# Cross attention: the attention result is split into two f16 parts by rows and transposed by the DMA crossbar, not by TensorE

## The reference, cut to what matters

```
q = x_norm @ wq.T ; k_new = x_norm @ wk.T ; v_new = x_norm @ wv.T
k = concat([ctx, k_new]) ; v = concat([ctx, v_new])
attn = softmax(q @ k.T * 512 ** -0.5)
out = attn @ v                    # (queries, 512)
x = x + out @ wo.T
```

## Time and profile before

| | |
|---|---|
| median of 3 runs | 1349.93 us (1348.22 to 1350.03) |
| the profiled execution | span 1349.0 us from first to last instruction |
| PE / DVE / ACT / POOL busy | 1327.4 / 1019.0 / 514.4 / 384.2 us |
| PE share of the span | 98% |
| mean DMA rate over the span | 90 GB/s |

### The profile page before, as it was taken

One profiled execution on the slowest core, in us unless ns is written; L12 is line 12 of the kernel. 1 busy time (PEld: TensorE's weight loads), 2 busy tenths in 40 slices (PEclk: granted clock), 3 DMA queues, 4 the chain that ended last, 5 costly groups with the idle time before them and its releaser, 6 DMA issues. The chain is left out here.

```text
span 1349.0 us, 23490 instructions
## 1 busy us (share of the span) xinstructions
PE 1327.4 (98%) x9232; PEld 773.9 (57%) x9232; DVE 1019.0 (76%) x2336; ACT 514.4 (38%) x1268; POOL 384.2 (28%) x304
## 2 busy tenths in 40 slices
PE   8999999999999999999999999999999999999998
PEld 6666666646666666666666666654444434444443
DVE  7444444269988888887888878858999798689594
ACT  4333333253333334343343334320001476666661
POOL 0000000012333222332223322313043296757571
PEclk9999999999999999999999999999999999999999
DMA  9555544541100220012210124155661000000002
GB/s 344 211 207 204 203 188 188 219 179 48 33 21 28 64 64 32 17 32 63 64 32 17 32 64 156 38 140 170 147 234 63 1 1 1 1 0 7 26 1 94
DMA packets 41766, 122.57 MB, mean 91 GB/s; under 512 B 4280, under 2 KB 6968, under 8 KB 34232
## 3 DMA queue, kind: packets, MB, share of 16 engines
q1 hardware_dynamic: 40488, 118.19, 25.8%
q10 hardware_dynamic: 1168, 2.88, 1.0%
HBM read 95.89 MB, written 25.17 MB: 90 GB/s over the span
## 5 line engine op out<-in xcount | busy, mean ns | idle before, releaser
L191 PE MATMUL psum<-xt_hi,hqk_hi 128*128 128x512 f16 x512 | 194.4, 380 | 0.0
L192 PE MATMUL psum<-xt_lo,hqk_hi 128*128 128x512 f16 x512 | 194.0, 379 | 0.0
L193 PE MATMUL psum<-xt_hi,hqk_lo 128*128 128x512 f16 x512 | 194.0, 379 | 0.0
L919 POOL TENSOR_TENSOR hd_rotated<-hd_products 64x512 f32<-64x512 f32 x32 | 40.8, 1274 | 419.7 <-DVE hd_products L1181 419.7
L1576 POOL TENSOR_TENSOR ff_part<-ff_part 128x512 f32<-128x512 f32 x88 | 129.1, 1470 | 79.9 <-DVE ff_part L1708 79.4
L1708 DVE SCALAR_TENSOR_TENSOR ff_part<-psum,gu_scale,ff_part 128x512 f32<-128x512 f32 x176 | 122.6, 743 | 33.1 <-PE psum L1602 28.3
L193 PE MATMUL psum<-hd_wv_hi,xt_lo 128*128 128x256 f16 x512 | 139.6, 273 | 0.0
L192 PE MATMUL psum<-hd_wv_lo,xt_hi 128*128 128x256 f16 x512 | 139.6, 273 | 0.0
L191 PE MATMUL psum<-hd_wv_hi,xt_hi 128*128 128x256 f16 x512 | 139.6, 273 | 0.0
L1601 PE MATMUL psum<-xt_hi,gu 128*128 128x512 f16 x352 | 133.7, 380 | 3.3 <-DVE ff_part L1708 2.7
L1602 PE MATMUL psum<-xt_lo,gu 128*128 128x512 f16 x352 | 133.4, 379 | 0.0
(11 more groups left out here) (202 smaller groups left out, 3094.0 us busy)
## 6 DMA issues: line engine op xcount, KB each, us to landing
xa_kv_t<-in_ctx_t_dram SPq DMA_DIRECT2D x16, 1024.0 KB, 5.4
xa_kv<-in_ctx_dram SPq DMA_DIRECT2D x16, 1024.0 KB, 4.9
w_rows<-in_head_weights_dram SPq DMA_DIRECT2D x10, 1024.0 KB, 8.5
z_scratch<-hd_z_hi SPq DMA_DIRECT2D x32, 256.0 KB, 2.6
z_scratch<-hd_z_lo SPq DMA_DIRECT2D x32, 256.0 KB, 3.3
hqk_lo<-z_scratch SPq DMA_DIRECT2D x8, 1024.0 KB, 7.5
w_rows<-z_scratch SPq DMA_DIRECT2D x8, 1024.0 KB, 8.0
xn<-in_x_dram SPq DMA_DIRECT2D x8, 512.0 KB, 4.1
```

The source lines that it names most:

```text
L191: pe.matmul(out, lh, rh, start=(first and i == 0), stop=False)
L192: pe.matmul(out, lh, rl, start=False, stop=False)
L193: last = pe.matmul(out, ll, rh, start=False, stop=(final and i == k - 1))
```

## The change

`att` (f32) is gone; `by_row_hi` and `by_row_lo` (f16, by rows, 128 x 2 x 512) take its place. ACT copies the bank of `attend` with the scale straight to f16 (`by_row_hi`), DVE computes bank times scale minus `by_row_hi` to f16 (`by_row_lo`) from the same bank and is now the one that marks it as moved. The constant AS is multiplied into `inv_total` by an added small DVE instruction for each half. SP then issues for each half two DMA transposes, SBUF to SBUF, 128 x 512 f16 (128 KB) each, `by_row_hi` to `att_hi` and `by_row_lo` to `att_lo`, ahead of that half's load of `kv`; they count on `att0_turned` or `att1_turned`, for which `project_out` waits. `turn_att`, the bank unit `turn` and ACT's `att_hi` copies are gone; ACT's two copies of v stand together.

```
--- before.py
+++ after.py
@@ -230,7 +230,7 @@
         own_hi, own_lo = sb("own_hi", [P, 2, P], F16), sb("own_lo", [P, 2, P], F16)
         top, low_top = sb("top", [P, 2], F32), sb("low_top", [P, 2], F32)
         total, inv_total = sb("total", [P, 2], F32), sb("inv_total", [P, 2], F32)
-        att = sb("att", [P, 2, D], F32)
+        by_row_hi, by_row_lo = sb("att_by_row_hi", [P, 2, D], F16), sb("att_by_row_lo", [P, 2, D], F16)
         att_hi, att_lo = sb("att_hi", [P, 2, KD, P], F16), sb("att_lo", [P, 2, KD, P], F16)
         x1 = sb("x1", [P, 2, 2, D], F32)
 
@@ -245,6 +245,7 @@
         x1_t_hi_done = sem("x1_t_hi_done")
         v_hi_done, probs_t_done = sem("v_hi_done"), sem("probs_t_done")
         inv_ready, att_hi_done = sem("inv_ready"), sem("att_hi_done")
+        att_turned = [sem("att0_turned"), sem("att1_turned")]
         identity_loaded, zeros_set = sem("identity_loaded"), sem("zeros_set")
 
         turn_x = [(("x", i), 6 + i) for i in range(2)]
@@ -253,7 +254,7 @@
         body = [(("scores", p), p) for p in range(2)] + [(("q", i), 2 + i) for i in range(2)] + \
             [(("probs", p), 4 + p) for p in range(2)] + [(("k", i), 6 + i) for i in range(2)] + \
             [(("att", p), p) for p in range(2)] + [(("v", p), 2 + p) for p in range(2)] + \
-            [(("turn", p), 4 + p) for p in range(2)] + [(("x", i), 6 + i) for i in range(2)] + \
+            [(("x", i), 6 + i) for i in range(2)] + \
             [(("out", p), 4 + p) for p in range(2)]
         banks = Banks(nc, ctx, "xa", before, body)
 
@@ -293,6 +294,10 @@
 
             def load_residual(j):
                 sp.dma_start(x1[:, j % 2, :, :], rows_of(x_rows, j * HALF_TILE, HALF_TILE)).then_inc(res_loaded[j % 2], 16)
+
+            def turn_att(p):
+                for by_row, to in ((by_row_hi, att_hi), (by_row_lo, att_lo)):
+                    sp.dma_start_transpose(to[:, p, :, :], by_row[:, p, :]).then_inc(att_turned[p], 16)
 
             def load_head_rows(i):
                 sp.dma_start(w_rows[:, i % 2, :], head_weights[block_of(i), :]).then_inc(rows_loaded[i % 2], 16)
@@ -341,9 +346,10 @@
                     for i in range(2):
                         banks.wait_filled(sp, *turned(NH - 1, i))
                     sp.dma_start(xn[:, :, :], rows_of(x1_rows, 0, TILE)).then_inc(first_x1_loaded, 16)
-                if not last_tile:
-                    for p in range(2):
-                        banks.wait_filled(sp, j, ("att", p))
+                for p in range(2):
+                    banks.wait_moved(sp, j, ("att", p))
+                    turn_att(p)
+                    if not last_tile:
                         load_kv(j + 1, p)
                 if j + 4 < NH:
                     for i in range(2):
@@ -446,16 +452,9 @@
                                          kv[:, p, 2 * s + i, :], start=False, stop=(i == 1), skip_group_check=True)
                 banks.fills(last, j, unit)
 
-            def turn_att(j, p):
-                unit = ("turn", p)
-                banks.wait_moved(pe, j, ("att", p))
-                banks.wait_room(pe, j, unit)
-                for k in range(KD):
-                    last = pe.transpose(psum[:, banks.bank(j, unit), block_of(k)], att[:, p, block_of(k)], ident[:, :])
-                banks.fills(last, j, unit)
-
             def project_out(j, p):
                 unit = ("out", p)
+                pe.wait_ge(att_turned[p], 32 * (j + 1))
                 banks.wait_room(pe, j, unit)
                 banks.fills(three_passes(pe, psum_of(j, unit), cols(att_hi[:, p, :, :], att_lo[:, p, :, :], slice(0, P)),
                                          weight(3, slice(0, D))), j, unit)
@@ -506,8 +505,6 @@
                     attend(j, p)
                 if not last_tile:
                     project_v(j + 1, 0)
-                for p in range(2):
-                    turn_att(j, p)
                 if not last_tile:
                     project_v(j + 1, 1)
                 if j + 2 < NH:
@@ -584,17 +581,12 @@
                 head_hi(j)
                 for p in range(2):
                     unit = ("att", p)
-                    act.wait_ge(inv_ready, 2 * j + p + 1)
+                    act.wait_ge(inv_ready, 2 * (2 * j + p + 1))
                     banks.wait_filled(act, j, unit)
-                    banks.moves(act.activation(att[:, p, :], psum_of(j, unit), ACT.Copy, scale=inv_total[:, p:p + 1]), j, unit)
+                    act.activation(by_row_hi[:, p, :], psum_of(j, unit), ACT.Copy, scale=inv_total[:, p:p + 1]).then_inc(att_hi_done, 1)
                 if not last_tile:
-                    move_v(j + 1, 0)
-                for p in range(2):
-                    banks.wait_filled(act, j, ("turn", p))
-                    act.activation(att_hi[:, p, :, :].rearrange("p a b -> p (a b)"), psum_of(j, ("turn", p)), ACT.Copy,
-                                   scale=AS).then_inc(att_hi_done, 1)
-                if not last_tile:
-                    move_v(j + 1, 1)
+                    for p in range(2):
+                        move_v(j + 1, p)
                 if j + 2 < NH:
                     for i in range(2):
                         first_half(j + 2, i)
@@ -672,6 +664,8 @@
                 for p in range(2):
                     banks.wait_moved(dve, j, ("scores", p))
                     dve.reciprocal(inv_total[:, p:p + 1], total[:, p:p + 1]).then_inc(inv_ready, 1)
+                    dve.wait_ge(inv_ready, 2 * (2 * j + p) + 1)
+                    dve.tensor_scalar(inv_total[:, p:p + 1], inv_total[:, p:p + 1], AS, None, ALU.mult).then_inc(inv_ready, 1)
                 if not last_tile:
                     move_qk(j + 1, 0, 1)
                 for p in range(2):
@@ -691,10 +685,10 @@
                 if not last_tile:
                     head_lo(j)
                 for p in range(2):
+                    unit = ("att", p)
                     dve.wait_ge(att_hi_done, 2 * j + p + 1)
-                    banks.moves(dve.scalar_tensor_tensor(att_lo[:, p, :, :].rearrange("p a b -> p (a b)"), psum_of(j, ("turn", p)), AS,
-                                                         att_hi[:, p, :, :].rearrange("p a b -> p (a b)"), ALU.mult, ALU.subtract),
-                                j, ("turn", p))
+                    banks.moves(dve.scalar_tensor_tensor(by_row_lo[:, p, :], psum_of(j, unit), inv_total[:, p:p + 1],
+                                                         by_row_hi[:, p, :], ALU.mult, ALU.subtract), j, unit)
                 if not last_tile:
                     for p in range(2):
                         move_v(j + 1, p)
```

2 lines of the change are left out of this document (added).

## The result

The changed kernel took 1357.36 us (median of 4 runs, 1355.97 to 1358.33), the kernel before 1349.70 (4 runs, 1348.22 to 1350.03): a ratio of 1.0060, 95% interval 1.0049 to 1.0072. It is 7.7 us slower, where 4.3 us less was forecast. The profiled execution has a span of 1354.8 us against 1349.0, so the traces have 5.8 us of it to show.

The account below looks back on a forecast made before the run. TensorE, busy for 98% of the span, was taken as the bound: -6.1 us in tiles 0 to 6 and +1.8 in the last tile make -4.3, from 1349.9 to 1345.6 us. The range was 1343.9 to 1368.

Parts of the forecast that it names:

- What bounds the kernel, and what goes: TensorE is busy throughout a tile; eight transposes removed save 0.87 us a tile, 6.1 us in tiles 0 to 6.
- The price of a transpose, m: Time one 128 KB DMA transpose adds to a train, in the queue or SP's issue, whichever is longer; taken as 0.8 us.
- my own formula: Half 1's transposed pair in tile 1 lands at 93.2 + 4m, so at 96.4 for m = 0.8.
- The bound at which half 1 becomes late, 0.95: Tiles 0 to 6: half 1's pair is in time for TensorE's output projection up to m = 0.95 us.
- rival B: In tiles, half 1 partly late: m 1.0 to 1.2, or dear last tile; +0.5 us, 1350.4, at m=1.1; chance 0.21.
- A: Transposing DMAs hidden in tiles 0 to 6, m up to 1.0: -5.1 to -2.5 us, point 1345.6; chance 0.43.
- What is queued behind on SP: SP's queue: kv loads come some 4 and 5 us late, wanted some 30 us on; input rows wait anyway: nothing.
- What is won there stays won: Behind the cross attention TensorE is the bound again, so the 4.3 us won there is kept.
- The last tile: Last tile: half 0's pair lands at 287.4, +0.9 us; four more matmuls at the low clock, 0.9 us; together +1.8.
- DVE and ACT: Each tile: ACT loses two copies, DVE gains some 0.5 us; both idle around them, so nothing; `by_row_lo` 0.64 us each.
- C: SP's queue becomes the bound: half 1's pair holds the output projection from m=1.17; +18 us at m=1.7; chance 0.28.
- D: In SP's queue each 128-column block is its own transfer, one after another; m 5.6 or more, about 1490 us; chance 0.08.

Follow-up runs that it names:

- experiment 2: Changed kernel, but SP issues both halves' pairs of transposes ahead of both kv loads; 1351.72 us, ratio 1.0027 to the kernel before.
- experiments 9 to 12: On experiment 3, each transposed part in two pieces, 1376.48 us, or four, 1465.86; one joined transpose per half: on the changed kernel 1349.46, on experiment 3 1345.81.
- experiment 1: Changed kernel, but in the last tile SP issues the next phase's v weight loads ahead of the transposes; 1353.51 us, ratio 1.0032 to the kernel before.
- experiment 4: Kernel before, with only the last tile's two v weight loads made late, behind a wait for the first output bank; 1355.85 us, ratio 1.0055.
- experiment 12: On experiment 3, one DMA transpose of 128x1024 per half in place of two of 128x512; 1345.81 us, ratio 0.9965 to the kernel before.
- experiment 8: On experiment 3, each pair of transposes in tiles 0 to 6 preceded by the same two into a spare buffer; 1377.26 us, ratio 1.0206.
- experiment 7: On experiment 3, the last tile's attention result transposed by TensorE as in the kernel before; 1344.45 us, ratio 0.9968 to the kernel before.
- experiment 3: Changed kernel with the edits of experiment 1 and experiment 2 together; 1347.08 us, ratio 0.9989 to the kernel before.

## Why the prediction was wrong, step by step

**What bounds the kernel, and what goes.** Right. TensorE is the bound in the tiles, and once nothing holds it the eight transposes are worth 0.87 us a tile (experiment 2: 5.24 us in six tiles).

**The price of a transpose, m.** The first of the two steps that failed, a mis-sized term: 0.8 taken. SP's issue is 1.25 us, and the landing of half 1 in tile 1, put into my own formula from the real start (88.01 + 4.9 + 4m = 97.4), gives m = 1.12. The bound at which half 1 becomes late, 0.95, was right: by the formula it is late by 4(1.12 - 0.95) = 0.7 us, and 0.64 is measured. This made 5.3 of the 6.1 us vanish. It is rival B's mechanism and about its size (-1.9 in seven tiles at m = 1.1; -0.8 measured), not A, which I took. Why it was mis-sized: I scaled m with bytes from plain stores. It is an issue price, the same per instruction from 32 to 256 KB (experiments 9 to 12), so no scaling of bytes could give it. I named SP's issue as a possible cost and gave it no value but a plain copy's.

The Trainium skill had it closer. "VectorE: DVE Perf Modes", section The three transpose paths, has 1309 ns for a 128x128 block, from which my estimate for overlapping blocks was m = 1.3. The section does not say what the figure spans; of a 128x128 piece here the issue took 1.23 us, which is near it, and issue to landing 2.4, which is not. The traces add that SP's issue of a transfer eight times as large is hardly dearer (1.23 to 1.32). "Advanced Engine Details and Errata", section X-Bar Transpose, which says transposing DMAs are as fast as regular ones, does not hold at this size: 1.25 us of issue against some 0.32 to 0.6 us for a plain transfer, and DMA engines 0.66 and 0.49 busy in the two windows shown.

**What is queued behind on SP.** The second step that failed, and with nearly as much in it. I listed the loads of `kv` and the input rows as behind the moved step, and for tiles 0 to 6 that costs nothing, as said. I did not go on to the last tile, where the same program order has the next phase's v weight loads (L362) behind the transposes and 3 MB ahead of the `x1` stores. Forecast nothing, measured +4.8 us in the trace; taken away alone (experiment 1) it gives 3 to 4 us back, and put alone into the kernel before (experiment 4) it costs 7.0. The program's order on SP has those loads right behind the new wait. Without this step the traces would differ by some 1 to 2 us (-0.8 and +2.6, less what comes back at 980), hardly to be told from no change: the mis-sized m took the gain away, and the queue made the kernel slower. "What is won there stays won" failed with it, for the next phase starts from what SP has stored.

**The last tile.** The mechanism was right, a wait for the pair and a longer stretch at the low clock: +1.8 forecast, +2.6 measured. The clock's part came as forecast (four more slow matmuls, 0.8 us, where I had 0.9); the wait's part was 1.8 us and not 0.9, the mis-sized m once more. That the wait for half 0 ended at 287.55, within 0.2 us of the forecast 287.4, is luck: its pair was issued at 283.73, 0.7 us earlier than I had it, and took 3.8 us and not 3.0. I also had the wait for `xn` only grow by what the transposes leave; it did (1.53 to 3.03).

**DVE and ACT.** Right, no wait of TensorE on either is new in tiles 0 to 6. The low part took 0.74 us, not 0.64, and half 0's pair was issued at 88.01, forecast 88.3.

**The rivals.** The result lies on C's side, but C's mechanism (m over 1.17, half 1 held by more than 0.87 us) came in at most in the tiles with the longest waits, 0.76 us, and by less than 0.1 us; D (each block 1.4 us or more in turn) did not either. No rival had the queue behind SP's wait.

What stays open: the trace accounts for 5.8 us and the medians differ by 7.7. The runs of one kernel spread by 2 to 8 us, so I leave the rest there. Part of that spread is TensorE's clock: in the last tile of the profiled execution of the kernel before it fell to 0.50, and in experiment 4, where TensorE's instructions are the same, it did not, and the tile's last matmul comes 1.7 us sooner. The terms of the ledger for the last tile and the next phase are one execution's, and can differ by as much in another. At the 385 GB/s of the earlier trace rows 3 MB need 8.2 us, an estimate, so a head start of 5.8 us is too short for them; that it still costs 4.2 us is more than the 2.4 missing, and no run shows why.

## What to carry to other kernels

A step put into an in-order queue with a wait of its own must be followed through every iteration, the last one above all, where what comes behind it is no longer the loop's own slack but the next phase's loads. A DMA transpose costs SP some 1.25 us whatever its size here: issue few and large ones (join parts in one buffer), start them before large loads of the same queue, and price the train by instructions, not bytes. Where TensorE waits anyway, leave its transposes in place; they cost nothing there.

## What the runs showed of the hardware that was not expected

- The issue of a DMA transpose on SP, medians but for the last: 1.23 us for 128x128, 1.25 for 128x256, 1.20 to 1.28 for 128x512 and 1.23 to 1.32 for 128x1024 (SBUF to SBUF, f16); landing 2.4, 2.4, 2.5 and 3.1 us after the issue began. The last number from the page of experiment 12 (count, median us to landing):

```profile
xa_att<-xa_att_by_row SPq DMA_TRANSPOSE x16, 3.1
```

- In experiment 8 a wait of 2.45 us on TensorE in the middle of tile 1 is followed by some 3 us at the 1.2 GHz level and so costs 4.3 us, while the changed kernel's waits of 0.47 to 0.76 us in tiles 0 to 6 are followed by none (clock 1.00). The length of the wait alone does not settle it. The 3.0 us for `xn` in the last tile are followed at once by the low level in the changed kernel (granted clock 0.50 in 284 to 286) and not in experiment 1 (1.00 until 288); the 1.5 us by it in the kernel before and not in experiment 4 (1.00 in 284 to 288); and in experiment 7 waits of 0.8 and 0.6 us early in the last tile are (0.50 in 268 to 271).
- The start of the program differs between executions of the same code. Granted clock in the first 20 us, and tile 0's first store of `x1`: 0.83 and 64.71 us (experiment 3), 0.91 and 63.67 (experiment 2), 1.00 and 62.84 (experiment 7); all three have the same work up to there. The span of one profiled execution therefore carries up to some 2 us that have nothing to do with the edit.
